# Last attention of a four-block kernel: the order of scores, values and weights in TensorE's queue

## What is computed

```
x = x + attention with rope (gn(x))            # stage A
x = x + selective scan block (gn(x))           # stage B
x = x + attention with relative positions(gn(x))  # stage C
x = x + neighbourhood attention (gn(x))        # stage D
```

```
qkv = (x @ w_qkv).reshape(B, H, W, 3, 12, 16)      # 12 heads of 16
q = q * 16 ** -0.5
kg, vg = the 7 x 7 window of k and v around each token (clipped at the edges)
attn = softmax(q . kg)                             # over the 49 neighbours
o = sum of attn * vg
return o @ w_out
```

## Time and profile before

| | us |
|---|---|
| median of 3 runs | 8146.06 |
| lowest and highest | 8145.80 and 8158.58 |
| the profiled execution, its own time | 8145.44 |
| its span, first to last instruction | 8143.6 |
| busy in the span: PE | 6816.9 (84%) |
| DVE | 5332.9 (65%) |
| ACT | 3280.9 (40%) |
| POOL | 1335.0 (16%) |
| mean granted clock of PE | 0.901 |

### The profile page before, as it was taken

One profiled execution on the slowest core, in us unless ns is written; L12 is line 12 of the kernel. 1 busy time (PEld: TensorE's weight loads), 2 busy tenths in 40 slices (PEclk: granted clock), 3 DMA queues, 4 the chain that ended last, 5 costly groups with the idle time before them and its releaser, 6 DMA issues. The chain is left out here.

```text
span 8143.6 us, 86925 instructions
## 1 busy us (share of the span) xinstructions
PE 6816.9 (84%) x32664; PEld 2753.3 (34%) x32664; DVE 5332.9 (65%) x5598; ACT 3280.9 (40%) x3610; POOL 1335.0 (16%) x804
## 2 busy tenths in 40 slices
PE   5999999977777777776767999999999999788877
PEld 1222222213233232332322444444444443333333
DVE  5777777758777686777866666666666664444444
ACT  2555555543223333232332444444444444333333
POOL 0111111104343343433423000000000000000001
PEclk8999999988787787877878999999999999888898
DMA  2111111110000000000000111111111110322222
GB/s 68 52 52 51 51 51 48 47 35 0 8 0 8 8 0 8 8 0 8 0 4 18 36 35 32 38 36 32 38 36 32 39 30 18 95 78 80 71 77 61
DMA packets 151437, 283.40 MB, mean 35 GB/s; under 512 B 46885, under 2 KB 52253, under 8 KB 151019
## 3 DMA queue, kind: packets, MB, share of 16 engines
q1 hardware_dynamic: 140267, 257.77, 10.8%
q0 software_dynamic: 10752, 20.08, 0.9%
HBM read 165.87 MB, written 89.79 MB: 31 GB/s over the span
## 5 line engine op out<-in xcount | busy, mean ns | idle before, releaser
L932 DVE TENSOR_REDUCE mx<-ring 128x1 f32<-128x1024 f32 (+1 forms) x1920 | 2172.0, 1139 | 901.5 <-PE ring L677 376.7
L828 ACT ACTIVATE pt<-ring 128x1024 f32<-128x1024 f32 (+1 forms) x1920 | 1868.6, 981 | 2183.4 <-PE ring L703 1060.0
L1534 POOL TENSOR_TENSOR hc<-hs,crep 128x1024 f32<-128x1024 f32 x384 | 980.1, 2552 | 1663.2 <-DVE hs L1490 1573.8
L727 PE MATMUL px<-pt,vo 128*32 128x512 f32 (+3 forms) x8064 | 1190.2, 580 | 7.6 <-ACT pt L828 7.5
L674 PE MATMUL ring<-kb,qb 96*128 96x512 bf16 x3072 | 1076.7, 392 | 117.8 <-ACT pt L828 38.8
L701 PE MATMUL ring<-qb,kb 99*128 99x512 bf16 x3072 | 1071.9, 390 | 26.8 <-DVE mx L932 13.6
L1229 PE MATMUL ring<-duh,spread 96*128 96x512 f32 x1536 | 647.8, 535 | 347.2 <-DVE hs L1479 215.4
L1490 DVE TENSOR_TENSOR_SCAN hs<-ring,hs 128x1024 f32<-128x1024 f32 x384 | 874.6, 2278 | 2.1 <-ACT ring L1377 2.1
L677 PE MATMUL ring<-hot,rq 128*128 128x512 f32 x1536 | 803.2, 582 | 0.0
L1377 ACT ACTIVATE ring<-ring,arow 128x1024 f32<-128x1024 f32 x384 | 416.0, 1083 | 955.1 <-PE ring L1218 955.1
L703 PE MATMUL ring<-rq,hot 128*128 128x512 f32 x1536 | 800.6, 581 | 0.0
(11 more groups left out here) (172 smaller groups left out, 6564.4 us busy)
## 6 DMA issues: line engine op xcount, KB each, us to landing
qk_parts<-part SPq DMA_DIRECT2D x192, 192.0 KB, 2.4
qb<-qk_parts SPq DMA_DIRECT2D x192, 96.0 KB
kb<-qk_parts SPq DMA_DIRECT2D x192, 96.0 KB
ocm<-os SPq DMA_DIRECT2D x576, 32.0 KB
rb<-reciprocals POOLq DMA_DIRECT2D x288, 64.0 KB, 2.5
qb<-qk_parts SPq DMA_DIRECT2D x192, 64.0 KB
kb<-qk_parts SPq DMA_DIRECT2D x192, 64.0 KB
qk_split<-hi SPq DMA_DIRECT2D x32, 384.0 KB, 3.5
```

Source lines behind the costliest of these rows:

```text
L727: last = nc.tensor.matmul(m.px[32 * g:32 * g + 32, h % 2, lo - f * HF:hi - f * HF], m.vo[img % 2][:, t, VW * head:VW * head + VC], pt[:, l ...
L828: nc.scalar.activation(pt, ps, ACT.Exp, scale=1.0 if L == "C" else HD ** -0.5).then_inc(s.pt, 1)
L932: nc.vector.tensor_reduce(out, ps, AX.X, ALU.max).then_inc(s.mx_used, 1)
L1534: nc.gpsimd.tensor_tensor(m.hc[i % HCS][:], m.hs[i % HSS][:], m.crep[k % 2][:], ALU.mult).then_inc(s.hc, 1)
```

## The change

In each turn of stage D the values of unit g - 1 are issued between the scores of unit n and the weights of unit g. Before, they stood behind the weights. Stages A and C keep their order (`L != "D"`), and so do all queues but PE's.

```diff
@@ attn_tensor, the loop over turns n
         g = n - lead
         if L != "D" and g % 2 == 1 and 3 <= g <= total + 1:
             values(*divmod(g // 2 - 1, steps // 2))
+        if L == "D" and 1 <= g <= total:
+            values(*divmod(g - 1, steps))
         if 0 <= g < total:
             weights(g)
-        if L == "D" and 1 <= g <= total:
-            values(*divmod(g - 1, steps))
```

## The result

| | before | after |
|---|---|---|
| median, us | 8147.17 (6 runs, 8145.78 to 8158.58) | 8181.83 (6 runs, 8171.33 to 8190.80) |
| ratio, 95% interval | | 1.0038 (1.0026 to 1.0050) |
| profiled execution, its span | 8145.44, 8143.6 | 8176.31, 8174.2 |
| first to last weights of stage D | 1117.9 | 1144.1 |
| mean granted clock in that stretch | 0.89 | 0.92 |

The changed kernel is 34.7 us (0.4%) slower. The forecast was 8226, 80.6 above the profiled execution of before, with a range from 8118 to 8345. The direction and the range held; the size was more than twice what came.

A forecast was written before the change was run, and what follows sets the result against it. The prediction took plain turns as PE's own work and plain heads as paced by SP's late `nm`. Start +28.2, after stores +28.2, end +36.8 and other stretches -12.6 summed to +80.6: 8226 us, range 8118 to 8345.

The forecast's parts named there:

- What bounds the kernel, and the new wait: Stage D plain turns: values wait for their own exponential, turns 2.30 us instead of 1.61, or 3.30 at clock 0.50.
- So once down, it stays down until a job or projection fills PE.: Stage D: after a long wait the clock sticks at 0.50, since each turn there waits 0.4 us; chance 0.56.
- start, 25 turns: Start of stage D to the first job: all turns at clock 0.50, 82.5 us against 54.3, +28.2.
- end, 27 turns: From head 89, without any job: all turns at clock 0.50, 89.1 us against 52.3, +36.8.
- five turns after each of six stores: Head after each image's store to the next job: clock 0.50, 16.5 us against 11.8, +28.2 over six.
- seven job regions: Stretches with jobs: values go into existing waits, against a slow first job; -0.8 us each.
- seven times five plain heads: Plain heads: slower turns replace the `nm` wait, -1.4 us each stretch, plus +2.5 on average for clock falls.
- seven times turns with projections and store: Three plain turns, projections and the store wait: half-clock turns go, one projection's values are hidden; -2.1 us each.
- one fall in every fourth stretch of plain heads: Plain heads: in one stretch of four the clock falls halfway, 10 turns x 1.0; +2.5 us on average.
- in between: Rival for stage D: the clock comes back after some eight turns; 8172 us, chance 0.13.
- Low also in plain turns: Rival for stage D: the clock falls in plain turns too; +241, 8387 us, chance 0.16.
- Quick return: Rival for stage D: the clock comes back as quickly as before, in two turns; 8125 us, chance 0.15.

The follow-up runs named there:

- e1: Changed kernel, but with values of unit g-2 instead of g-1 ahead of weights; stage D 1074.0 us, ratio to before 0.9963.
- e3: Changed kernel with the stage D exponential applied to only half of each tile; stage D 1065.3 us, ratio to before 0.9953.
- e4: Kernel before the change with the stage D exponential applied to only half of each tile; stage D 1116.6 us, ratio to before 1.0006.
- e9: Changed kernel with each stage D exponential issued in four pieces; stage D 1340.5 us, ratio to before 1.0273.
- e8: Changed kernel with the transposition (L684) moved behind values, ahead of weights; stage D 1139.7 us, ratio to before 1.0046.
- e10: Changed kernel with each stage D exponential issued in eight pieces; stage D 1465.1 us, ratio to before 1.0432.
- e2: Changed kernel with the second scores matmul of each stage D unit issued three times; stage D 1116.7 us, ratio to before 1.001.
- e6: Changed kernel with `nm` issued ahead of the loads on SP in stage D; stage D 1122.8 us, ratio to before 1.0022.
- e5: Kernel before the change with `nm` issued ahead of the loads on SP in stage D; stage D 1048.4 us, ratio to before 0.9943.

## Why the prediction was right or wrong

**What bounds the kernel, and the new wait: right.** 2.30 us a turn at 1.00 was forecast, 2.29 came; 3.30 at 0.50, 3.33 came; more than 300 waits of 0.6 or 0.4 us, 306 came. e1, e3 and e4 show that the wait for L828 is the cause. That nothing waits for `nm` any more in plain heads was right too: 9.15 us a head where 9.2 was forecast.

**What is left of the long waits: smaller than forecast.** The waits for `nm` came to 40.0 us, 8 times, where about 60 and 10 were forecast. Those behind the six stores were to stay over 5 us and came as 3.7 to 4.7, and the one ahead of the end, said to be of the same kind, came as 1.7. The rows had only shown that 1.32 leaves the clock up and 3.43 doesn't, so the term for the end had a fall at its start only by luck. Nor is 1.32 a bound: within 2 us of a wait of 1.25 in the job region the clock fell in two images (at 7073.9 and 7370.9), for 3.4 us each.

**The step that failed: "So once down, it stays down until a job or projection fills PE."** By stretches, in us:

| | forecast | came |
|---|---|---|
| start, 25 turns | +28.2 | +7.3 (54.2 to 61.5) |
| end, 27 turns | +36.8 | +18.5 (52.3 to 70.8) |
| five turns after each of six stores | +28.2 | +28.8 (72.2 to 101.0) |
| seven job regions | -5.6 | -10.4 |
| seven times five plain heads | +7.7 | -9.3 |
| seven times turns with projections and store | -14.7 | -8.6 |
| stage D | +80.6 | +26.2 |
| ahead of it and behind it | 0 | +4.4 |

The rows add up to 26.3; the difference is rounding. Start and end make 39.2 of the 54.4 us that were too much in stage D. There the clock came back after 13.3 and 10.2 us of turns that wait 0.37. The evidence I leaned on was one stretch of stage A, 17.9 us at 0.50 with waits of 0.10: I read it as "any gap keeps the clock down". The waits of 0.10 were not the only ones there. In the trace of before the clock is at 0.50 from 103.7 to 134.4, with these inside:

```profile
113.04 6.69 PE L674 MATMUL ring<-kb,qb 96*128 96x512 bf16 x12 [6.62 <-DVE mx L932]
121.05 0.37 PE L684 MATMUL ring<-ident,mx 128*8 128x128 f32 x1 [1.32 <-DVE mx L932]
...
124.72 2.17 PE L674 MATMUL ring<-kb,qb 96*128 96x512 bf16 x4 [0.74 <-DVE mx L932]
```

From the end of the last of these to the clock's return lie 9.7 us, and 17.9 us, too, lies within the 10 to 27 us that the return takes in stage D. So the stretch could not tell "delayed" from "held". e9 comes nearest to holding, at 0.55 in 3.52, and even there the clock came back twice.

After the stores the term was exact (+28.8 for +28.2), but in part by luck. The five turns take 16.95 us and the first job starts 17.8 after their first weights. In five images the clock was back only 19.2 to 23.7 us after these weights, so a return after 10 or 13 us, as at the start and the end, would have made the term smaller. In the sixth image it was back after 14.9, ahead of the job, with PE's turns up to there the same as in the other five (three waits of 0.37, then a turn whose wait L433 and L684 fill). In e8 it was back ahead of the job after five of six stores. There too the clock was late, not held.

**A second allowance that failed:** one fall in every fourth stretch of plain heads, +2.5 x 7 = 17.5 us. There was none. Without it the term is 7.7 - 17.5 = -9.8, and -9.3 came. In before, 26 of the 35 plain heads have some time at 0.50, and each fall within them lies in a wait for `nm` or at most 2 us behind its end; with those waits gone the falls went too.

**At the very end** 27 turns at 3.30 were forecast and 70.8 us came. In the last turns no scores stand between weights and values, so the wait is 0.90 us, and there the clock, after 41.0 us at 1.00, fell and stayed down through the 18.2 us to the last weights.

**The rivals.** What came lies nearest to "in between" (8172, which had 0.13). Its terms for start and end, +11.2 and +17.8, came as +7.3 and +18.5, and +28.2 behind the stores as +28.8. "Low also in plain turns" (8387) is what e9 and e10 do. "Quick return" is closest to e2, in whose start the clock was back in two turns: ratio 1.001. (The terms given for "quick return" add up to -20.4, not -20.6; nothing hangs on it.)

The Trainium skill (TensorE: Matmul & The Clock Gate, A second HAM failure mode) tells of frequent short idle times under which the clock goes back and forth. The changed kernel's plain heads don't show it (0 of 35 with time at 0.50); e9's, with 22 of 35 and two returns within them, come nearer to it.

`nm` lands 4.9 to 6.5 us after its last issue in plain heads of the changed kernel, behind the loads; with the loads issued after it (e6) it lands after 1.8 us in 31 of 35 plain heads and after 2.1 at most. The Trainium skill (DMA: Bandwidth & Descriptors, Anatomy of one DMA) gives about 2.0 us as a DMA's fixed cost, for the path of DMAs issued from GpSimd; e6 agrees with it for these two, issued from SP. What the page's figure alone leaves out is the loads ahead, and e5 shows what they cost.

**What stays open:** why the return took 13.3, 10.2, 16.3 and 27.3 us at start and end, and 14.9 to 23.7 behind the stores, in turns that are much alike, and why e6 gains more around the stores than I can account for.

## What to carry to other kernels

Before a consumer is moved closer to its producer, count what stands between them in that queue; here 0.40 us of scores cannot hide 0.81 us of exponential, while the same move with a distance of two units (e1) gains. If a DMA wait hides an engine's slack, mend the queue of the DMA first and compare orders then: the two orders lay 26 us apart with the late `nm` and 74 without it, and both mended together gave 1%. A short stretch in which the clock stayed low says that the return takes at least that long, not that it never comes; and before the gaps between matmuls are blamed, the longer waits in the same stretch have to be looked for.

## What the runs showed of the hardware

- Small differences in a wait that every turn has decided between two clocks: with 0.60 us in 2.29 none of 35 plain heads had time at 0.50, with 0.79 in 2.48 22 of them, with 1.05 in 2.73 34. Once down, with 0.37 in 3.33 the return took between 10.2 and 27.3 us; with 0.55 in 3.52 the clock stayed down for 84.7 us and more at the start, but was back after 3.4 and 20.5 in two other places.
- PE work that lies in a wait can save time: two more matmuls in each turn (e2) made stage D 27 us shorter, by the clock alone.
- Pieces of an exponential overlap on ACT: the half took 0.49 us, the whole 0.81, a quarter 0.33, and four quarters only 0.19 us more than the whole by PE's wait. I had expected 0.5.
- Two small writes on SP (`nm`) landed 1.8 us after the last issue with nothing just ahead of them (e6), and 4.9 to 6.5 us behind four loads (the changed kernel).
- Kernels that agree up to stage D reached it at times 24.7 us apart (6992.9 to 7017.6), as much as the change itself costs. Differences have to be read inside the stage.
